# A four-layer graph network on one core: transfers of 125 partitions issued as 112 and 13

## The reference

```python
edge_index = jnp.stack([src, dst])
h = jnp.maximum(_layernorm(x), 0.0)
x = x + L0(h, edge_index, edge_type_8, ...)      # relu([h_src, h_dst, onehot] @ W1 + b1) @ W2 + b2, summed by dst
h = jnp.maximum(_layernorm(x), 0.0)
x = x + L1(h, edge_index, edge_attr_16, ...)     # 4-head attention over edges, softmax by dst
h = jnp.maximum(_layernorm(x), 0.0)
x = x + L2(h, edge_index, ...)                   # normalized sum of neighbours @ W, relu
h = jnp.maximum(_layernorm(x), 0.0)
x = x + L3(h, edge_attr_64, edge_attr_9, ..., edge_index)   # 8-head attention with tensor products, batch norm
return x
```

## Time and profile before

| | us |
|---|---|
| median of 3 runs | 3109.23 |
| lowest, highest | 3104.41, 3112.86 |
| the profiled execution | 3103.95 |
| its span, first to last instruction | 3102.2 |
| TensorE busy | 2460.4 (79%) |
| VectorE busy | 2187.5 (71%) |
| GpSimd busy | 2033.7 (66%) |
| ScalarE busy | 868.7 (28%) |

### The profile page before, as it was taken

The page is one execution under the profiler, slowest core; times in us unless marked ns, Lnnn a source line. Parts: engine busy times, 40 slices in busy tenths (PEclk is TensorE's granted clock), DMA queues, the critical chain, the costliest instruction groups (busy, mean ns, idle before and its releaser), DMA issues. The chain is left out here.

```text
span 3102.2 us, 51526 instructions
## 1 busy us (share of the span) xinstructions
PE 2460.4 (79%) x14042; PEld 2123.0 (68%) x14042; DVE 2187.5 (71%) x5057; ACT 868.7 (28%) x2421; POOL 2033.7 (66%) x2116
## 2 busy tenths in 40 slices
PE   5877777525766667477787767999999999999997
PEld 4777777424666666355565556888888888888884
DVE  4655555526888888555555564788888888888885
ACT  1111111136666664111111111223222233222233
POOL 4777777457777771177777745777777776767730
PEclk9777777657888888599989987999999999999996
DMA  3443333133333330044545456988889888898850
GB/s 85 94 93 87 86 86 85 31 65 65 59 60 61 61 56 7 29 153 153 162 153 161 153 150 162 219 213 206 206 206 213 208 206 203 209 211 208 202 137 11
DMA packets 333728, 404.37 MB, mean 130 GB/s; under 512 B 171120, under 2 KB 202974, under 8 KB 333538
## 3 DMA queue, kind: packets, MB, share of 16 engines
q1 hardware_dynamic: 252002, 251.19, 34.8%
q0 software_dynamic: 66560, 96.41, 14.0%
q10 hardware_dynamic: 14976, 54.53, 5.1%
HBM read 339.81 MB, written 62.07 MB: 130 GB/s over the span
## 5 line engine op out<-in xcount | busy, mean ns | idle before, releaser
L1935 PE MATMUL psum<-ckv,z 128*128 128x256 f32 x4160 | 968.2, 383 | 0.0
L1935 PEld LDWEIGHTS psum<-ckv,z 128*128 128x128 f32 x4160 | 766.9, 191 | 98.0
L1770 POOL DMA_INDIRECT acc<-QW,dst_i x416 | 400.2, 962 | 183.6 <-issue 111.2
L234 POOL DMA_INDIRECT ga<-TA,src_i x416 | 409.5, 984 | 160.8 <-issue 126.5
L1780 POOL DMA_INDIRECT ga<-XX,src_i x416 | 400.5, 963 | 163.8 <-issue 122.3
L1027 POOL DMA_INDIRECT ga<-T,src_i x416 | 402.5, 968 | 152.7 <-issue 125.9
L234 POOL DMA_INDIRECT ga<-T,src_i x416 | 399.2, 960 | 149.3 <-issue 124.3
L2052 DVE TENSOR_TENSOR z<-psum,shb 128x2560 f32<-128x2560 f32 x104 | 293.2, 2820 | 67.8 <-PE psum L1926 67.5
L1121 PE MATMUL psum<-HT,wy 128*128 128x128 f32 x1664 | 260.2, 320 | 69.0 <-DVE wy L1394 68.8
L445 PE MATMUL psum<-wre,re 128*128 128x68 f32 x832 | 208.6, 342 | 132.7 <-DVE oneT L290 80.9
L1121 PEld LDWEIGHTS psum<-HT,wy 128*128 128x128 f32 x1664 | 238.3, 228 | 87.1 <-DVE wy L1394 80.9
(11 more groups left out here) (366 smaller groups left out, 4198.2 us busy)
## 6 DMA issues: line engine op xcount, KB each, us to landing
shb<-in_ea SPq DMA_DIRECT2D x104, 640.0 KB
WKV<-wkvo ACTq DMA_DIRECT2D x104, 512.0 KB
shb<-in_ea SPq DMA_DIRECT2D x104, 512.0 KB
wkv<-WKV SPq DMA_DIRECT2D x104, 512.0 KB
dl<-DL SPq DMA_DIRECT2D x208, 128.0 KB
win<-TB SPq DMA_DIRECT2D x416, 32.0 KB
ga<-T,src_i POOLq DMA_INDIRECT x832
ef<-in_ea SPq DMA_DIRECT2D x104, 128.0 KB
```

Source lines behind the costliest of these rows:

```text
L234: pool.indirect_dma_start(o, None, table, bass.IndirectOffsetOnAxis(ap=src_i[:, g * GT + t:g * GT + t + 1], axis=0)).then_inc(s_g[k], 16)
L1770: pool.indirect_dma_start(qg[:, (g % QR) * GT + t, :], None, QW, bass.IndirectOffsetOnAxis(ap=dst_i[:, g * GT + t:g * GT + t + 1], axis=0) ...
L1935: last = pe.matmul(kv_of(k)[:, t, :], z[:, k % 2, j, t * 128:(t + 1) * 128], ckv[:, j, :], start=(j == 0), stop=(j == NZ - 1))
```

## The change

A helper issues a transfer as two, partitions 0 to 111 and partitions 112 to 124, one after the other on the same queue and the same semaphore, which therefore rises by 32. Every load or store of 125 partitions but the final one goes through it: 15 transfers become 30. Each wait for one of them waits for twice the amount. Nothing else moves; TensorE, VectorE, ScalarE and GpSimd have the instructions that they had, in the same order. Line numbers of the changed kernel are 6 higher from the helper on.

```diff
+        ROWS = (slice(0, 112), slice(112, PN))
+
+        def put_rows(eng, o, i, s):
+            for P in ROWS:
+                eng.dma_start(o[P], i[P]).then_inc(s, 16)
...
-                pool.wait_ge(n0_oa, len(PARTS) * 16)
+                pool.wait_ge(n0_oa, len(PARTS) * 32)
...
-                sp.dma_start(X[:], A["x"].rearrange("(p j) f -> p j f", p=PN)).then_inc(l_x, 16)
+                put_rows(sp, X, A["x"].rearrange("(p j) f -> p j f", p=PN), l_x)
...
-                    sp.dma_start(TA.rearrange("(p j) f -> p j f", p=PN)[:, J_of(part), :], ta[:, J_of(part), :]).then_inc(n0_oa, 16)
+                    put_rows(sp, TA.rearrange("(p j) f -> p j f", p=PN)[:, J_of(part), :], ta[:, J_of(part), :], n0_oa)
...
-                sp.dma_start(T1.rearrange("(p j) f -> p j f", p=PN), trow[:]).then_inc(n1_o, 16)
+                put_rows(sp, T1.rearrange("(p j) f -> p j f", p=PN), trow, n1_o)
                 sp.wait_ge(n1_dve, LOOPS)
-                sp.dma_start(T1W[0:N, :].rearrange("(p j) f -> p j f", p=PN), dwb[:]).then_inc(n1_o, 16)
-                sp.wait_ge(n1_o, 3 * 16)
+                put_rows(sp, T1W[0:N, :].rearrange("(p j) f -> p j f", p=PN), dwb, n1_o)
+                sp.wait_ge(n1_o, 5 * 16)
...
-                sp.dma_start(T2.rearrange("(p j) f -> p j f", p=PN), yn[:]).then_inc(n2_o, 16)
-                sp.wait_ge(n2_o, 16)
+                put_rows(sp, T2.rearrange("(p j) f -> p j f", p=PN), yn, n2_o)
+                sp.wait_ge(n2_o, 32)
...
-                    sp.dma_start(XX.rearrange("(p j) f -> p j f", p=PN)[:, J, :], twice[:, J].rearrange("p j a f -> p j (a f)")).then_inc(n3_ox, 16)
+                    put_rows(sp, XX.rearrange("(p j) f -> p j f", p=PN)[:, J, :], twice[:, J].rearrange("p j a f -> p j (a f)"), n3_ox)
...
-                    sp.dma_start(QW.rearrange("(p j) f -> p j f", p=PN)[:, J_of(part), :], tab[:, J_of(part), :]).then_inc(n3_oq, 16)
+                    put_rows(sp, QW.rearrange("(p j) f -> p j f", p=PN)[:, J_of(part), :], tab[:, J_of(part), :], n3_oq)
```

More of the change, by code:

```diff
@@ L371, in _ @@
                     sp.wait_ge(n0_a, part[1])
-                    sp.dma_start(TA.rearrange("(p j) f -> p j f", p=PN)[:, J_of(part), :], ta[:, J_of(part), :]).then_inc(n0_oa, 16)
+                    put_rows(sp, TA.rearrange("(p j) f -> p j f", p=PN)[:, J_of(part), :], ta[:, J_of(part), :], n0_oa)
                 for part in PARTS:
                     sp.wait_ge(n0_b, part[1])
-                    sp.dma_start(TB[0:N, :].rearrange("(p j) f -> p j f", p=PN)[:, J_of(part), :], tb[:, J_of(part), :]).then_inc(n0_ob, 16)
+                    put_rows(sp, TB[0:N, :].rearrange("(p j) f -> p j f", p=PN)[:, J_of(part), :], tb[:, J_of(part), :], n0_ob)
                 sp.wait_ge(l_dl, 32)
@@ L389, in body @@
                     if isinstance(i, int) and k == 0:
-                        sp.wait_ge(n0_ob, len(PARTS) * 16)
+                        sp.wait_ge(n0_ob, len(PARTS) * 32)
                     window_loads(win, sp, i, k, TB, D, e0_w, e0_P, e0_sp)
@@ L522, in _ @@
                 c.mark(dve.tensor_copy(iota_p[:], iota_pi[:]))
-                dve.wait_ge(l_x, 16)
+                dve.wait_ge(l_x, 32)
                 ln = Chain(dve, n0_dve)
@@ L1774, in _ @@
                 groups = NT // GT
-                pool.wait_ge(n3_ox, len(HALVES) * 16)
+                pool.wait_ge(n3_ox, len(HALVES) * 32)
                 for g in range(groups):
@@ L1783, in _ @@
                         pool.wait_ge(n3_dve, NODE3)
-                        pool.wait_ge(n3_oq, len(PARTS) * 16)
+                        pool.wait_ge(n3_oq, len(PARTS) * 32)
                     if g:
```

## The result

| | before | after |
|---|---|---|
| median of 7 runs each, us | 3103.69 | 3083.51 |
| lowest, highest | 3101.47, 3112.86 | 3079.32, 3092.13 |
| the profiled execution, and its span | 3103.95, 3102.2 | 3079.32, 3077.6 |

The ratio is 0.9934, with a 95% interval from 0.9916 to 0.9952: 20.5 us less (the medians themselves lie 20.2 apart), faster by twice what a measurement of this kernel can tell. The forecast was 0.6% less and 3090.1, from a median of 3109.23 that four more runs lowered to 3103.69.

A forecast was written before the change was run, and what follows sets the result against it. Gathers in layers 0 to 2 and TensorE in layer 3 were taken as the bounds, passing earlier starts on whole. Five gains summed to 19.1 us, from 3109.23 to 3090.1, range 3080 to 3099.

The forecast's parts named there:

- load of x: At the kernel's start, x loads at 410 GB/s and LayerNorm starts near 6.1 us: gain 4.3 us, bounds 3.3 to 5.2.
- TA: Before layer 0's gathers, the last part of TA's store lands sooner: gain 0.8 us, between 0.3 and 1.3.
- T1, T1W: At the block's end T1 is gone before T1W is issued, so T1W alone decides: gain 5.2 us, bounds 4.6 to 5.8.
- T2: Store before layer 2's gathers: ScalarE's copies become last, so 0.95 us of a possible 4.3 is gained, bounds 0.5 to 1.0.
- XX, QW: Layer 3's start: limited by TensorE's query table (8.1 us) and QW's store (7.7); 7.8 us taken, bounds 6.5 to 8.4.
- What bounds the kernel: Gathers every 1.3 us in layers 0 to 2 and full TensorE in layer 3 pass on whole any earlier start.
- How many engines: A transfer uses the largest number of engines up to 16 dividing its partitions; the fullest carries 8 rows instead of 25.
- a pair that serializes: Rival: 112 partitions still use few engines, each critical place pays a second issue, 2.2 us, ending at 3111.4; chance 0.05.
- 13 rows on one engine: Rival: 112 partitions use 16 engines but the fullest carries 20 rows of 25; gain 8 us, 3101; chance 0.03.
- The rate: Split transfers were taken to run at 410 GB/s for rows of 6 KB, 300 GB/s for TA's shorter rows.
- layer 3 gives part back: Rival: wide QW stores share engines with layer 3's first gathers, which land 4 us later, giving 3094; chance 0.10.
- the slower case: Rival in layer 3: TensorE's low clock stays granted longer; at 70 us of low clock the time is 3125; chance 0.03.

The follow-up runs named there:

- the repetition: The changed kernel timed again, unaltered, in five rounds on one chip beside the kernel before: median 3086.14 us, ratio 0.9936 (0.9924 to 0.9947).
- the copies taken away: Against the changed kernel, ScalarE's seven copies of layer 2's transposed table cut to one column each: 3087.91 us with T2's store whole, 3080.96 with it split.
- the kernel with five pieces: Against the changed kernel, each transfer in pieces of 32, 32, 32, 16 and 13 partitions in place of 112 and 13: 3087.65 us.

## Why the prediction held, and where it missed

| place | forecast, us | measured, us | from |
|---|---|---|---|
| load of x | 4.3 | 3.9 | LayerNorm's start |
| TA | 0.8 | 1.0 | 4.91 - 3.91 |
| T1, T1W | 5.2 | 5.1 | 11.72 - 6.61 |
| T2 | 0.95 | 0.14 | 8.79 - 8.65 |
| XX, QW | 7.8 | 7.6 | 22.18 - 14.56, the lead at the issue of XX |
| sum | 19.1 | 17.8 | |

**What bounds the kernel.** Held. Each stage passed its start on. The gathers, first to last start, before and after: 535.1 and 536.6 us, 528.0 and 526.9, 524.8 and 521.5, 1095.0 and 1092.6. The 6.8 us by which the span shrank beyond the five terms are such differences of stages and of what follows them (lead lost 0.9 in layer 0, won 1.2, 4.1 and 2.4 later), on lines that the change doesn't touch. They are no steady part of it: all kernels here together show 520.7 to 524.8 in layer 2, and the second profile of the changed kernel, with 6.6, 8.7 and 7.0 us behind the issues of T1, T2 and XX, has a span of 3086.3, 8.7 us more than the first. So the span of one profile shows the gain only roughly. The 17.8 us of the five places lie within the intervals of both measured ratios (14.9 to 26.1 us, and 16.5 to 23.6 in the repetition); how much of the 2 to 3 us between them and the medians is real isn't shown.

**How many engines.** Held for all: 0.95 to 1.04 with 112 + 13, and the other cuts followed the divisors. With that the rivals of a pair that serializes and of 13 rows on one engine are gone: the first would have kept 11.7 us at T1. The sentence of the Trainium skill against two transfers to partition halves ("DMA: Bandwidth & Descriptors", "Rules for kernel authors") doesn't hold for 125 partitions cut as 112 + 13, where 20.5 us were won; a cut into 64 and 61 loses 90.

**The rate.** Too high: 302 to 316 GB/s at T1 and T2 instead of 410. It cost little, since 850 KB take 2.7 instead of 2.1 us, and T1 has 3.1 us before T1W is issued. XX showed it openly, 6.9 us against a forecast 5.6, but stood off the path there. The load of x, with other loads behind it, was slower still:

```profile
1.50:4.50 3.00, 0.00 (x0) 0.00 (x0) 2.67 (x1) 0.58 (x1) 2.84 (x2) 1.00 0.90 252
```

At 252 GB/s 800 KB take 3.2 us instead of 1.95, yet LayerNorm was only 0.4 us later than forecast. So the 3.4 us that the forecast called fixed were some 0.8 us too long, and the two errors partly cancelled; that was luck.

**T1 and T1W.** Held: the next block starts at 639.16, which is 2.9 us behind the first issue of T1W at 636.28; forecast 2.8 to 3.2. The forecast's own terms, 0.47, 0.2 to 0.4 and 2.3, make 3.0 to 3.2 and a gain of 4.8 to 5.0, so its 5.2 came closer than its working. The first T1 gather is 9.1 us earlier than before, against a forecast 10.3, since layer 0 lost 0.9 of the lead.

**T2.** That ScalarE would be late next was right, as the copies taken away show. The step that failed is "the next block starts 0.32 us after an engine that is last". ScalarE ends at 1290.84 + 2.22 = 1293.06, and the next block starts at 1293.82, 0.76 later; without the copies it was 0.75. The 0.32 had been read behind VectorE. And the copies end 7.74 us behind the issue of T2, where before it was 7.37: the granted clock stayed at 0.50 (1.2 GHz) all through the block, where in the kernel before it had risen (0.50 up to 1299, 1.00 or 2.4 GHz from 1300 on), as this window of before shows, and TensorE's transposes are in that chain.

```profile
1299.00:1303.00 4.00, 2.37 (x13) 1.17 (x11) 0.28 (x2) 4.00 (x5) 0.00 (x0) 0.89 0.32 127
```

0.44 and 0.37 are the whole 0.81 us. The two can be told apart in the kernel with five pieces, where the clock did rise under the same copies (three rows of its timeline and a window):

```profile
1290.35 3.40 SPq L282 DMA_DIRECT2D T<-n_yn  x5
...
1293.67 4.05 ACT L1544 ACTIVATE acc<-psum 64x500 f32<-64x500 f32 x5 [0.21 <-PE psum L217]
...
1298.48 1.76 DVE L1683 MEMSET ef<- 64x2048 f32 x1 [4.40 <-PEq L1520]
...
1295.00:1296.00 1.00, 0.69 (x7) 0.43 (x6) 0.00 (x0) 1.00 (x2) 0.00 (x0) 1.00 0.00 0
```

There the copies end at 1297.72, again 7.37 us behind the issue, and the next block starts 0.76 us later, 8.13 behind it. So the 0.37 goes with the clock and the 0.44 doesn't, and with the risen clock this term would be 8.63 - 8.13 = 0.5 us. What makes the clock rise in one kernel's block and not in another's isn't shown. It isn't the cut of T2: with T2 whole the copies took 7.72 us as well.

**Layer 3.** Held. The z transposes start at 1868.68, 0.5 us behind the end of the last query product (1865.66 + 2.49; the row puts the 0.52 us down to ScalarE's copy of it), no longer behind the gathers; QW comes 21.84 us after XX was issued, forecast 22.3. (Of the two limits, 8.1 and 7.7, the prediction took "the smaller, 7.8", a slip of 0.1.) The rival in which layer 3 gives part back is gone: the third group of gathers still leads by 22.20, as much as the first transposes. TensorE does wait 5.23 us for it (4.66 before), but from an earlier start. So is the slower case: the mean granted clock of the profiled execution is 0.875 after 0.871.

## What to carry to other kernels

Look at the share of the DMA engines while a transfer is waited for, and at its partition count: a count with a small largest divisor up to 16 (125, 124, 61) leaves most engines idle, and a cut is good if the fullest engine then carries few rows in all (8 with 112 + 13, 9 with 120 + 5, but 32 with 124 + 1 and 65 with 64 + 61). What such a cut gives is worth reading at each place for itself, since the next thing that is late may come at once (T2) or only after some 8 us have been won (XX). A start in front of a stage that runs on one saturated engine is passed on whole, so such gains add up, and the short store at the very end is one of them.

## What the runs showed of the hardware

**The rate isn't the number of engines times a constant.** With one engine busy it was 26 GB/s, with five 127 to 132, so 26 for each; a store of 128 partitions on 16 reached 410, again 26. But 64 partitions on 16 engines reached 205, 32 on 16 211, 120 on 15 205, 100 on 10 202, 112 on 16 302 to 316, and 124 on four 95.

One reading fits nearly all of it, formed after the last run and so not tested. The Trainium skill, "SBUF — State Buffer", "Door 1: The DMA port swizzle", says that the memory has 16 ports, each for two groups of four partitions, p to p+3 and the same 32 higher, within each half of 64.
**The end of a block costs different amounts.** In layer 2's node block the next block starts 0.75 or 0.76 us behind ScalarE's last copy in all eight kernels where that copy is last, with one column or 500, at either clock. At the end of layer 0, where VectorE is last, it is 0.32 us, and 0.32 or 0.33 in the later kernels too. Why wasn't tried.
